# Linear-attention scores as two alternating 32-row tiles, fewer masked key copies, and rewritten issue orders in a decoder kernel

## What is computed

```python
q = _silu(to_heads(q)); k = _silu(to_heads(k)); v = to_heads(v)      # 16 heads, d = 16
diag_decay = exp(where(idx >= 0, -s * idx, -inf))
qk = einsum('bhmd,bhsd->bhms', qi, ki) * diag_decay
out = qkv_none_diag + einsum('bhms,bhse->bhme', qk, vi)
...
x = _layernorm(x + _L0_attn_ref(...)); x = _layernorm(x + _L0_xattn_ref(...)); x = _layernorm(x + _L0_ffn_ref(...))
x = _layernorm(x + _L1_attn_ref(...)); x = _layernorm(x + _L1_xattn_ref(...)); x = _layernorm(x + _L1_ffn_ref(...))
```

## Time and profile before

| what | us |
|---|---|
| median of 3 runs (930.47 to 934.96) | 934.71 |
| the profiled execution: its own time | 937.12 |
| its span, first to last instruction | 935.3 |
| TensorE busy | 845.0 |
| VectorE busy | 633.1 |
| ScalarE busy | 364.7 |
| GpSimd busy | 349.3 |

### The profile page before, as it was taken

The page is one execution under the profiler, slowest core; times in us unless marked ns, Lnnn a source line. Parts: engine busy times, 40 slices in busy tenths (PEclk is TensorE's granted clock), DMA queues, the critical chain, the costliest instruction groups (busy, mean ns, idle before and its releaser), DMA issues. The chain is left out here.

```text
span 935.3 us, 12349 instructions
## 1 busy us (share of the span) xinstructions
PE 845.0 (90%) x4548; PEld 632.7 (68%) x4548; DVE 633.1 (68%) x1218; ACT 364.7 (39%) x739; POOL 349.3 (37%) x337
## 2 busy tenths in 40 slices
PE   6898986788998999998999999997796999999996
PEld 5676754667536778876537878875134787738885
DVE  5342478998946278998944479996999877526222
ACT  5120345763273254443272354444384322261110
POOL 5300426851303047861312139840457521202221
PEclk9898997999998999999999999998789799999999
DMA  6202041023020244440020154321200123313542
GB/s 230 107 6 82 1 160 43 1 80 106 2 113 1 82 159 136 136 134 15 2 112 1 34 159 136 113 93 46 91 1 1 35 68 109 129 35 116 165 140 74
DMA packets 26927, 76.10 MB, mean 81 GB/s; under 512 B 3436, under 2 KB 5420, under 8 KB 26228
## 3 DMA queue, kind: packets, MB, share of 16 engines
q1 hardware_dynamic: 26612, 75.26, 24.2%
q10 hardware_dynamic: 256, 0.07, 0.0%
HBM read 74.13 MB, written 1.11 MB: 80 GB/s over the span
## 5 line engine op out<-in xcount | busy, mean ns | idle before, releaser
L915 PE MATMUL B<-late 128*128 128x256 f32 (+2 forms) x1064 | 243.1, 382 | 2.0 <-POOL late L698 1.1
L915 PEld LDWEIGHTS B<-late 128*128 128x128 f32 (+1 forms) x1064 | 199.4, 193 | 32.7 <-POOL late L698 2.0
L1599 DVE TENSOR_TENSOR_SCAN arena<-F,arena 128x512 f32<-128x512 f32 x128 | 149.1, 1206 | 3.3 <-POOL arena L590 2.4
L599 POOL TENSOR_TENSOR arena<-du,arena 128x1024 f32<-128x1024 f32 x60 | 140.9, 2358 | 23.1 <-PE F L915 23.1
L842 ACT ACTIVATE F<-delta,a_neg 128x255 f32<-128x255 f32 x256 | 109.3, 467 | 54.0 <-DVE arena L1599 53.7
L698 POOL TENSOR_TENSOR late<-late 128x512 f32<-128x512 f32 x42 | 53.5, 1275 | 137.4 <-DVE late L1744 101.7
L1609 DVE TENSOR_TENSOR arena<-arena,F 128x1024 f32<-128x1024 f32 x60 | 73.3, 1221 | 8.4 <-PE F L915 2.7
L579 POOL TENSOR_TENSOR rs<-ve,minus_half 128x2 f32<-128x2 f32 (+1 forms) x20 | 15.3, 764 | 165.6 <-DVE ve L1549 75.1
L904 ACT ACTIVATE late<-B 128x512 f32<-128x512 f32 x42 | 24.9, 593 | 93.7 <-PE B L915 93.6
L883 ACT ACTIVATE late<-B 128x512 f32<-128x512 f32 x96 | 51.9, 593 | 18.7 <-PE B L915 17.0
L915 PE MATMUL F<-arena,ident 128*128 128x256 f32 x232 | 57.9, 391 | 0.5 <-DVE arena L1637 0.5
(11 more groups left out here) (357 smaller groups left out, 1466.0 us busy)
## 6 DMA issues: line engine op xcount, KB each, us to landing
late<-in_w_moe SPq DMA_DIRECT2D x112, 384.0 KB, 3.5
room<-in_w_f SPq DMA_DIRECT2D x4, 2544.0 KB, 9.1
arena<-b_out SPq DMA_DIRECT2D x32, 256.0 KB, 5.5
room<-in_w_l SPq DMA_DIRECT2D x4, 768.0 KB, 6.4
w_m<-in_w_m SPq DMA_DIRECT2D x1, 2112.0 KB
room<-in_w_l SPq DMA_DIRECT2D x4, 512.0 KB, 3.7
x_t<-in_x_t SPq DMA_DIRECT2D x4, 256.0 KB, 2.6
x_tok<-in_x_tok SPq DMA_DIRECT2D x4, 256.0 KB, 5.3
```

The costliest lines, as they stand in the source:

```text
L599: g.tensor_tensor(state(n).rearrange("p d (s t) -> p d s t", s=2), du[:, 2 * dp:2 * dp + 2, :].unsqueeze(2).to_broadcast([P, 2, 2, S]), b_ ...
L915: return t_.matmul(dst, lhsT, rhs, start=start, stop=stop, skip_group_check=True)
L1599: v.tensor_tensor_scan(h, F[i][:, :], h, 0.0, ALU.mult, ALU.add)\
```

## The change

1. **Scores.** A head's 16 rows lie in a group of 32 rows with one other head. `kz` now has two copies, one for the even and one for the odd heads, and a matmul takes only the 32 rows of its group. The two heads of a pair always lie in different groups of 32 rows and go to different banks. Their matmuls alternate: first blocks of both, then second blocks of both. The waits of both heads stand ahead of the pair.
2. **Masks.** VectorE makes 2 copies per batch, not 8; `headmask` is by parity.
3. **Products of no use.** Tables name phases, banks and counts for all batches: in batch 0 `xa` 5, `xb` 3, `fa1` 2, `fd2` 8, `m2` 2, `bq3` 2; in batch 1 `ob` 1, `xa` 2, `xc` 3, `fa2` 3; in batch 3 `ba2` 1. That is 32 for 26.
4. **Orders.** All numbers of `FILL` and `LATER` are new.

```diff
 FILL = {
...
-    "POOL": {"at1": 1, "ob": 1, "xc": 3, "xd": 1, "fa1": 2, "fa2": 1, "fg3": 4, "fg4": 3, "fg5": 7, "fd1": 1,
-            "m1": 2},
+    "POOL": {"at6": 1, "xb": 2, "fa1": 3, "fa2": 2, "fg0": 5, "fg5": 3, "fd1": 4, "fd2": 3, "m1": 3},
 }
...
-IDLE_FIRST = {"xa": 7, "fa1": 19}
+SPIN_FRONT = {"ob": 0, "xa": 3, "xb": 3, "xc": 2, "fa1": 2, "fa2": 2, "fa3": 2, "fd1": 0, "fd2": 0, "m2": 3, "m3": 0}
+SPIN_BACK = {"bq3": 2, "ba2": 0, "br2": 1, "br3": 1}
+SPIN = [{"xa": 5, "xb": 3, "fa1": 2, "fd2": 8, "m2": 2, "bq3": 2}, {"ob": 1, "xa": 2, "xc": 3, "fa2": 3}, {},
+        {"ba2": 1}]
...
-        self.kz = words[:, 0:4096].rearrange("p (f v t) -> p f v t", f=KT, v=8)
+        self.kz = words[:, 0:1024].rearrange("p (f c t) -> p f c t", f=KT, c=2)
...
-                    spin(K[0], IDLE_FIRST.get(ph, 0))
+                if ph in SPIN_FRONT:
+                    spin((pl.F if ph in FRONT_A else F)[SPIN_FRONT[ph]], SPIN[b].get(ph, 0))
...
                     for n in (2 * i, 2 * i + 1):
-                        f, v = divmod(head(n), 8)
                         if n < 3:
                             pe.wait_ge(*[df.at("qs", b), df.at("ks", b), af.at("vz1", b)][n])
                         else:
                             pe.wait_ge(*(af.at(f"c{n - 3}", b) if n % 2 == 0 else df.at(f"a{n - 3}", b)))
-                        pe.wait_ge(*df.at(f"kz{v}", b))
-                        bank = pl.F[(n + 1) % 3]
-                        qf = pl.qs.rearrange("p (f t) -> p f t", f=KT)
-                        mm(bank[:, 0:S], pl.kz[:, f, v, 0:P], qf[:, f, :], True, True)
-                        mm(bank[:, S:S + P], pl.kz[:, f, v, P:S], qf[:, f, P:S], True, True)\
-                            .then_inc(pf.step(f"s{n}"), 1)
+                        pe.wait_ge(*df.at(f"kz{head(n) % 2}", b))
+                    qf = pl.qs.rearrange("p (f t) -> p f t", f=KT)
+                    for t in range(TT):
+                        for n in (2 * i, 2 * i + 1):
+                            f, v = divmod(head(n), 8)
+                            r = slice(v // 2 * 32, v // 2 * 32 + 32)
+                            c = slice(0, S) if t == 0 else slice(S, S + P)
+                            last = mm(pl.F[(n + 1) % 3][:, c], pl.kz[r, f, v % 2, t * P:t * P + P], qf[r, f, t * P:S],
+                                      True, True)
+                            if t == TT - 1:
+                                last.then_inc(pf.step(f"s{n}"), 1)
...
             def back(b, ph):
                 bk = home(b)
+                if ph in SPIN_BACK:
+                    spin(bk.K[SPIN_BACK[ph]], SPIN[b].get(ph, 0))
...
-                    for c in (0, 2, 4, 6, 1, 3, 5, 7):
+                    for c in range(2):
                         v.tensor_scalar(pl.kz[:, :, c, :], pl.ks.rearrange("p (f t) -> p f t", f=KT),
                                         headmask[:, c:c + 1], None, ALU.mult).then_inc(df.step(f"kz{c}"), 1)
...
-        (p // HD0 == np.arange(8)[None, :]).astype(f), (p % 32 == np.arange(32)[None, :]).astype(f),
+        (p // HD0 % 2 == np.arange(8)[None, :]).astype(f), (p % 32 == np.arange(32)[None, :]).astype(f),
```

## The result

The changed kernel takes 955.82 us (median of 4 runs, 953.53 to 961.04); the kernel before, on the same chip, 932.59 (929.38 to 934.96). The ratio is 1.0275, with a 95% interval from 1.0243 to 1.0308: it is **slower by 2.75%** (the medians alone, 23.2 us apart, give 2.5%). I had predicted 925.3 and a range up to 937. The profiled execution took 956.82 us, its span 955.0, against 935.3 before.

What follows compares the result with a forecast made beforehand. TensorE bounds the experts and batch 1's linear attention, VectorE those of batches 2 and 3; batch 0's ends on GpSimd. 1.3 + 0.7 + 4.8 + 2.6 + 0 = 9.4 us off 937.1 gives 927.7, median 2.4 lower: 925.3; range 910 to 937.

Steps and rivals of the forecast that it cites:

- The loop of 1.56 us: Linear attentions, per pair of heads: pair 0.70, to VectorE 0.18, its work 0.63, back to TensorE 0.05; before, 1.40.
- the gains of batches 0 and 1: Linear attentions: batch 0's last average earlier, gain 1.3 us; batch 1 gains 0.7 us, from m2 that stood behind.
- VectorE binds: Linear attentions of batches 2 and 3: VectorE is the bound, so TensorE's 5.6 us saved per batch buy nothing.
- the first rival: Attentions: clock falls from half-filled rows and waiting TensorE; slower, up to 942.6 us; chance 0.12 for all, 0.09 for some.
- The wait itself: Score pairs: both heads wait first, one needing the even head of the pair just before; 1.56 us per pair against 1.40.
- Row tiles overlap: Score matmuls: two row tiles run at once, so a pair takes 0.70 us instead of 1.40.
- the 1.04 us of loads one by one: Score pairs: if loads of different row groups go one by one, a pair costs at least 1.04 us; total 929.4.
- The second rival: Score matmuls: tiles don't overlap, pair stays 1.40, 933.7 us; or loads one by one, 929.4; chance 0.12 for both.
- Masks, 4.8 us: Batches 2 and 3, VectorE's full stretch: six fewer masks save 2.4 us per batch, 4.8 in all.
- The orders, "nothing, 4 us to either side": Changed FILL and LATER, rest of the expert phases: worth nothing, with 4 us to either side for the range.
- Batch 3's order, 2.6 us: Batch 3, u and sres ahead of the query split: first maximum at 653.4, gain 2.6 us, 4 if clock high.
- Products, "nothing": Moved products of no use: gain 1.7 us from eight ahead of fd2, loss 1.7 from clock at 56 us; sum nothing.

Runs made afterwards that it cites:

- e4: Kernel before with eight masked copies and 128-row matmuls, but both waits ahead of each pair and the two heads' blocks alternating: 942.06 us, ratio 1.0104.
- e7: Kernel before with the new scores and two masks, plus two 32-row products behind each pair in batches 0 and 1: 946.76 us, ratio 1.0151.
- e14: Changed kernel plus two 128-row products behind each pair of heads in batches 0 and 1: 944.90 us, ratio 1.0155 to the kernel before.
- e6: Kernel before with the new scores and two masks, plus two 128-row products behind each pair in batches 0 and 1: 934.75 us, ratio 1.0035.
- e5: Kernel before with 64-row score matmuls and four masked copies, each head behind its own wait: 929.95 us, ratio 0.9988.
- e9: Kernel before with all changed numbers of FILL and LATER, old scores and old products of no use: 939.90 us, ratio 1.0078.
- e8: Kernel before with only the changed table of products of no use: 936.77 us, ratio 1.0052.
- e15: Kernel before with the changed table of products of no use, without the eight ahead of fd2 of batch 0: 938.39 us, ratio 1.0084.
- e16: Kernel before with the changed third part of LATER, plus eight products ahead of fd2 of batch 0: 930.09 us, ratio 1.0004.
- e13: Kernel before with 64-row score matmuls, four masked copies, own waits, and the changed third part of LATER: 925.85 us, ratio 0.9948.
- e3: Kernel before with two masked copies and 32-row score matmuls, head after head, each behind its own wait: 938.72 us, ratio 1.0086.
- e12: Kernel before with only the third part of LATER changed (one back phase of VectorE moved behind m2): 926.30 us, ratio 0.9953.

## Why the prediction was wrong

**The step that failed first is that the sum has the attentions at the high clock.** The loop of 1.56 us, the gains of batches 0 and 1 and "VectorE binds" in batches 2 and 3 all rest on it; a fall stood only as the first rival. I gave that 0.12, on the ground that from 167 to 177 us TensorE was busy 5.65 of 10 us and the clock stayed. I had argued with busy time. e4 and e7 show that busy time is not what decides here: busy 69% with 128-row matmuls the engine kept the clock, busy 84% with 32-row ones it lost it. Nothing in the trace of before could show it, since it has no score matmul of 32 rows; the rival named the half-filled array, and I didn't weigh that as a cause of its own. Its size was right for batch 0 at most: it gave 3.2 us each in batches 0 and 1 and 4.6 in batches 2 and 3, for falls of 10.2 us. They were 23.9 us in batch 0, 17 in batch 1 and 20 in batch 2, both in two stretches, and 3.4 in batch 3, and the four attentions grew by 4.3, 7.9, 10 and 0.4 us. Keeping the clock in the first two is worth some 10.9 us (e14). Even with all of its falls the rival came to 942.6 only, since it left the scores' other costs, the orders and most of the products at nothing.

**The loop of 1.56 us: a term mis-sized.** It is 1.80 to 1.82. VectorE's 0.62 is as taken; the way back is 0.25, not the estimated 0.05, and from a pair's start to VectorE it is 0.95, not 0.88. "Batch 0 gains 1.3, batch 1 gains 0.7" turned into losses even at the high clock: in e6, with clock 1 in both, the attentions take 18.8 and 18.7 us from the first pair to the end of the last average, for 17.0 and 15.5 before. Its added products make the loop 1.91 us, so without them it would be somewhat less. The wait itself was named rightly; e4 prices it at 10.8 us for 128-row matmuls.

**Row tiles overlap: right.** A pair's eight instructions take 0.65 us from first to last start (105.11 to 105.76), for the 0.70 predicted, and 0.92 with the last one's tail; e4's eight of 128 rows take 1.55 by the same measure. The loads of 32 rows are hardly shorter: 184 ns in batch 1's first two pairs, at the high clock, for 193 of 128 rows, and 235 as the mean of the 192 of batches 0, 2 and 3, many of them at the lower clock. The trace agrees with the rule of the Trainium skill (TensorE: Matmul & The Clock Gate, LDWEIGHTS) that a load is timed by its columns.

```profile
L919 PEld LDWEIGHTS B<-late 32*128 32x128 f32 x16 | 1.4, 184 | 1.4 <-ACT late L724 1.1 <-DVE late L1443 0.3
L919 PEld LDWEIGHTS F<-arena 32*128 32x128 f32 x192 | 22.2, 235 | 21.2 <-issue 8.2 <-ACT arena L724 7.3 <-DVE arena L1443 4.2
```

The loads of the two heads start 0.01 us apart, so they overlap too, and the 1.04 us of loads one by one is out as well. The second rival is out.

**Masks, 4.8 us: the work went, the gain didn't come.** Two masks take 0.88 us, where eight took 3.26, and VectorE's busy time fell by 1.8 us from masks to last maximum in each late batch. But in batch 2 VectorE stopped being the bound (clock and order), and in batch 3 its window kept its length, 28.4 us for 28.0, with 2.6 idle. "TensorE's free time is worth nothing since VectorE binds" held only while TensorE kept its own pace. In e5 the masks' gain isn't in the median either.

**The orders, "nothing, 4 us to either side": wrong in size.** They cost 9.95 us (e9): 4.2 in `FILL`, 10.0 in the first two parts of `LATER`, and 3.7 won in the third. I had looked for orders in the expert phases, where TensorE has no idle time, and not among the maxima of the late attentions, where VectorE was busy 28.5 of 28.9 us: there any order of TensorE that feeds it less evenly must lose. 3.6 us of the 10 are located there in batch 2, and 3.2 in batch 3. The rest of them wasn't taken apart, nor what in `FILL` costs its 2.3 to 4.2.

**Batch 3's order, 2.6 us: right, and somewhat larger.** It is 9.9 us instead of 13.3 in the changed kernel too (661.08 + 5.27 to 676.23). The clock was high there, the case for which the prediction had 4. The third part of `LATER` alone makes the kernel 3.7 us faster.

**Products, "nothing": wrong by 6 us.** I took half of the full price of 3.4 us for the clock after the wait for `xb`. The clock did fall, at 60.31 us for 10.2 us in the changed kernel, for as long in e8 and for 13.7 us in e15. e15 says that the eight don't cost it. The gain of the eight was right in its place (the projection runs in 5.34 us for 8.41, from 98.10) and didn't show in the whole kernel (e16).

```profile
92.73 3.72 PE L919 MATMUL F<-rows,ident 128*128 128x256 f32 x16
...
98.10 5.34 PE L919 MATMUL B<-x_t,room 128*128 128x256 f32 x24
```

**The sum.** In place of -9.4 us: scores +17.3 (of it 13.7 that 128-row products give back), products +6.3, orders +9.95, together 33.5; measured 23.2. So some 10 us are counted twice. That a stretch of low clock can fall only once on the same work, and that an engine that is late hides the waits of the others, would explain it, but I didn't divide them.

## What to carry to other kernels

Before a matmul is cut to fewer rows, ask what keeps TensorE's clock: here small row tiles saved time per pair and took the clock from everything in the stretch, and busy time didn't warn of it. A test is cheap, two kernels that fill the same waits with full and with small products; read what the engine did before the clock fell, since behind the fall all work takes longer and any engine looks busy. And when an engine is busy 98% of a window, price every reordering on the engines that feed it first, not the work that is taken from it.

## What the runs showed of the hardware that I had not expected

- In the attentions the granted clock went by the rows of the matmuls more than by busy time: it fell to 0.5 behind 4.46 us in which TensorE was busy 3.76, all of it with scores and products of 32 rows in batch 1 (e7), and stayed at 1 where it was busy 3.09 of 4.46 with 128-row scores (e4), although in e4 seven eighths of the weight rows are zeros. The Trainium skill (TensorE: Matmul & The Clock Gate, What's actually happening) says that the clock follows how busy the engine has been; these runs differ from that, as far as busy time goes. The fall at `xb` in a wait of 8.05 us (e8) agrees with it. Nor do 128 rows always keep the clock: the kernel before lost it at 113.30 us, behind 6.8 us that were busy for 5.67. With 64 rows the clock stayed in e5's batches 0 to 2 and fell in batch 2 of e13.
- With 32 rows and little waiting it isn't certain either way: in e3 the clock fell in batch 0 and stayed in batch 1 of one execution, and its runs lie between 933.16 and 945.19 us.
- Two matmuls in different groups of rows overlap without being interleaved in the program, head after head: 32 instructions in 4.26 us (e3), where the same in 128 rows take 5.48, as in e12 at 97.04 us.
- A semaphore's way from VectorE's last product to TensorE's next matmul is 0.25 us (106.68 to 106.93), five times what I had taken.
